# First expert round: stream 0's sum and the head of the rope jobs begin five half tiles later, the head runs at 2.45 positions a half tile, and three gathers are set three positions apart

## The reference, cut to what matters

```
x = x + encoder(layernorm(x))        # 4 layers: attention with ALiBi mask, feed-forward; final layernorm
x = x + experts(layernorm(x))        # first round
x = x + rope_attention(layernorm(x))
x = x + experts(layernorm(x))        # second round

def experts(x):                      # 8 experts, each token goes to its best 2
    comb = softmax weight of each token's two experts, else 0
    h = gelu(x @ W1[e] + b1[e]);  y = h @ W2[e] + b2[e]
    return sum over e of comb[e] * y[e]
```

## Time and profile before

| | |
|---|---|
| median of 3 runs | 2651.41 us (2651.28 to 2651.97) |
| the profiled execution | 2659.2 us, its span 2657.4 us |
| mean granted TensorE clock | 0.932 |
| PE / DVE / ACT / POOL busy | 86% / 66% / 55% / 39% of the span |
| second group of the first round, with the head | some 170 us, to about 1944 us |

### The profile page before, as it was taken

The page is one execution under the profiler, slowest core; times in us unless marked ns, Lnnn a source line. Parts: engine busy times, 40 slices in busy tenths (PEclk is TensorE's granted clock), DMA queues, the critical chain, the costliest instruction groups (busy, mean ns, idle before and its releaser), DMA issues.

```text
span 2657.4 us, 102576 instructions
## 1 busy us (share of the span) xinstructions
PE 2277.5 (86%) x44398; PEld 1394.7 (52%) x44398; DVE 1755.3 (66%) x5525; ACT 1463.5 (55%) x2646; POOL 1037.8 (39%) x1261
## 2 busy tenths in 40 slices
PE   3689999999999999999998888996878778888983
PEld 1345555555555555555554444785644444436872
DVE  6877777777777777777877774422567777852212
ACT  0357677777677777777655556442245434454441
POOL 6334333333334333333444545423334554442135
PEclk9799999999999999999988988998888888889997
DMA  4253333342433333333222211575622222205773
GB/s 115 81 161 101 109 120 117 105 132 93 121 107 105 124 105 116 109 128 93 87 68 62 75 33 34 185 220 147 177 67 70 65 64 62 64 13 173 224 205 109
DMA packets 162531, 288.76 MB, mean 109 GB/s; under 512 B 28504, under 2 KB 116312, under 8 KB 160344
## 3 DMA queue, kind: packets, MB, share of 16 engines
q1 hardware_dynamic: 153696, 264.23, 33.0%
q0 software_dynamic: 8384, 17.97, 2.5%
HBM read 227.33 MB, written 95.96 MB: 122 GB/s over the span
## 4 chain that ended last, share of the span: by engine, by line
PE 61%; DVE 19%; ACT 7%; issue 4%; POOL 3%; SPq 2%; DMA 2%; another core or an unknown queue 2%; POOLq 0%; ACTq 0%; DVEq 0%
PE bank L481 23%; PE bank L647 9%; PE bank L601 9%; DVE mx L1281 6%; PE bank L787 5%; PE bank L797 5%; PE bank L665 3%; ACT big L878 3%; PE bank L488 2%; DVE xn L973 1%; DVE stats L960 1%; ACT OT L884 1%; PE bank L609 1%; ACT big L946 1%
## 5 line engine op out<-in xcount | busy, mean ns | idle before, releaser
L878 ACT ACTIVATE big<-bank 128x512 f32<-128x512 f32 x1600 | 919.8, 599 | 704.5 <-PE bank L481 662.5
L1281 DVE TENSOR_REDUCE mx<-bank 128x16 f32<-128x512 f32 (+1 forms) x1440 | 903.0, 654 | 417.1 <-PE bank L609 385.0
L1577 POOL TENSOR_SCALAR_AFFINE_SELECT big<-big 128x768 f32<-128x768 f32 (+1 forms) x640 | 392.9, 637 | 915.5 <-ACT big L878 915.1
L481 PE MATMUL bank<-QS,KS 99*32 99x512 bf16 (+3 forms) x10240 | 651.6, 312 | 46.1 <-ACT big L878 35.3
L601 PE MATMUL bank<-KS,QS 96*32 96x352 bf16 (+15 forms) x10240 | 592.5, 294 | 103.2 <-DVE mx L1281 63.4
L647 PE MATMUL bank<-big,V 128*9 128x512 f32 (+3 forms) x5120 | 457.8, 453 | 19.0 <-POOL big L1577 10.7
L601 PEld LDWEIGHTS bank<-KS,QS 96*32 96x32 bf16 x10240 | 243.1, 99 | 410.7 <-issue 177.3
L481 PEld LDWEIGHTS bank<-QS,KS 99*32 99x32 bf16 x10240 | 218.0, 99 | 220.4 <-ACT big L878 94.0
L609 PE MATMUL bank<-mask_a,ident_b 128*32 128x64 bf16 (+1 forms) x5760 | 305.8, 196 | 0.8 <-issue 0.5
L946 ACT ACTIVATE big<-bank,big 128x256 f32<-128x256 f32 x368 | 150.7, 471 | 253.4 <-PE bank L787 198.8
L647 PEld LDWEIGHTS bank<-big,V 128*9 128x9 f32 x5120 | 130.8, 92 | 154.7 <-issue 86.2
(11 more groups left out here) (216 smaller groups left out, 2727.4 us busy)
## 6 DMA issues: line engine op xcount, KB each, us to landing
big<-e_pack SPq DMA_DIRECT2D x92, 578.0 KB
QS<-part_scr SPq DMA_DIRECT2D x480, 96.0 KB
KS<-part_scr SPq DMA_DIRECT2D x480, 96.0 KB
part_scr<-parts SPq DMA_DIRECT2D x80, 384.0 KB
x_rows<-in_alibi SPq DMA_DIRECT2D x47, 384.0 KB, 4.9
y_rows<-in_alibi SPq DMA_DIRECT2D x47, 384.0 KB, 5.6
big<-x_rows SPq DMA_DIRECT2D x92, 128.0 KB
y_rows<-big SPq DMA_DIRECT2D x92, 128.0 KB
```

The costliest lines, as they stand in the source:

```text
L481: last = mm(out[c:c + 32], stationary[:, c:c + 32], moving, start=start, stop=stop)
L878: A(dst, src, ACT.Exp).then_inc(exp_done, 1)
L1281: v.tensor_reduce(mx[:, quad, k, 0:w], src, axis=AX.X, op=ALU.max).then_inc(a_used, 1)
L1577: g.affine_select(out=blocks, in_=blocks, compare_op=ALU.is_ge, fill=0.0, base=0, pattern=[[0, n], [1, P]], channel_multiplier=-1).then_in ...
```

## The change

Five numbers. The head's lag goes from 8 to 13 half tiles and its rate from 2.1 to 2.45 positions a half tile; stream 0's sum and layernorm go from q = 7 to q = 12; the gathers of streams 1, 2 and 3 begin at positions 12, 30 and 12 where they began at 15, 36 and 16, with three positions from pair to pair where there was one.

```diff
-HEAD_LAG, HEAD_RATE = 8, 2.1
+HEAD_LAG, HEAD_RATE = 13, 2.45
...
-        COMBINE_FROM, COMBINE_EVERY, COMBINE_BESIDE = (7, 12), (6, 6), (1, 4)
+        COMBINE_FROM, COMBINE_EVERY, COMBINE_BESIDE = (12, 12), (6, 6), (1, 4)
...
-        GATHER = {1: (-2, 15, 1), 2: (-2, 36, 1), 3: (-1, 16, 1), 4: (0, 16, 5), ...
+        GATHER = {1: (-2, 12, 3), 2: (-2, 30, 3), 3: (-1, 12, 3), 4: (0, 16, 5), ...
```

More of the change, by code:

```diff
@@ L431, in hybrid_kernel @@
         ROUTE = ENC - JOBS
-        COMBINE_FROM, COMBINE_EVERY, COMBINE_BESIDE = (7, 12), (6, 6), (1, 4)
+        COMBINE_FROM, COMBINE_EVERY, COMBINE_BESIDE = (12, 12), (6, 6), (1, 4)
         GATHER_BESIDE = {1 + 6 * S + at: (S, k) for S in range(5) for k, at in enumerate((0, 1, 3, 4))}
         COMBINE = {1: (-2, 27), 2: (-1, 8), 3: (-1, 28), 4: (1, 15), 5: (2, 15), 6: (3, 15), 7: (4, 15)}
-        GATHER = {1: (-2, 15, 1), 2: (-2, 36, 1), 3: (-1, 16, 1), 4: (0, 16, 5), 5: (1, 18, 5), 6: (2, 18, 5), 7: (3, 18, 5)}
+        GATHER = {1: (-2, 12, 3), 2: (-2, 30, 3), 3: (-1, 12, 3), 4: (0, 16, 5), 5: (1, 18, 5), 6: (2, 18, 5), 7: (3, 18, 5)}
         def spread(j):
```

## The result

| | kernel before | changed kernel |
|---|---|---|
| median of the comparison, us | 2650.18 (2641.03 to 2651.97, 6 runs) | 2632.49 (2629.34 to 2637.97, 6 runs) |
| ratio, 95% interval | | 0.9943 [0.9924, 0.9962] |
| profiled execution, its span, us | 2659.2, 2657.4 | 2633.4, 2631.6 |

The change is faster by 15.1 us (0.0057 x 2650.2; interval 10.1 to 20.1). The forecast was 2645.1 with a range from 2638.0: the direction was right, the size less than half of what came, and the median lies 5.5 us under the range. Two later groups of runs gave 0.9932 for the same kernel.

The account below looks back on a forecast made before the run. PE was taken to be held by a 15.63 us wait for stream 0's sum, then by idle times before and behind the first scores; 9.3 - 2.0 - 4.0 - 0.9 + 3.9 = 6.3 us saved, 2645.1 us, range 2638.0 to 2651.5.

Parts of the forecast that it names:

- fifth term: Behind the first scores: fewer gathers of streams 2 and 3 beside dense work save 3.9 us, ends 0 and 7.5.
- 12.4 - 8.5 = 3.9: Two rows of eight priced 12.4 us; rows of six, four and two priced 4.9, 2.5 and 1.1; saving 3.9.
- third term: From L488 to the first scores: the front gets no shorter, so 3.7 us are given back plus 0.3, -4.0.
- fourth term: Ahead of the stacks' loads: ten gathers in one row, two more than before, cost a third of 2.5 us, -0.9.
- first, five half tiles into the hole: PE's idle time before L488: five half tiles of 1.87 us run inside the wait for stream 0's sum, +9.3 us.
- second, the sum begins later: Stream 0's sum on DVE: three more tiles' biases and a later gather landing start it 2.0 us later, -2.0.
- the remaining 21.5: In the front, behind the bias ahead of the last split: splits, store, landing and loads keep their 21.5 us.
- Both new waits: In the denser head: the third projection waits for DVE's read, 0.9 us, and V for the fourth rotation, 1.3.
- about 6: Sign for the fifth term: idle times beside stream 2's and 3's gathers fall from 9.3 us to about 6.
- short rows are free: Rival, chance 0.15: only the row of six costs and the front gets shorter; 12.1 us saved, 2639.3.
- The gathers hold nobody back: Rival, chance 0.20: the stops belong to the stacks' loads, not the gathers; 3.8 us saved, 2647.6.
- The slower case, by full DMA engines: Rival, chance 0.07: crowded transfers cause the stops, stream 0's gather lands 8.3 us late; -5.5 us, 2656.9.

Follow-up runs that it names:

- e9: The kernel before with the head at rate 2.45 up to its first scores (two half tiles from front to rest); ratio 0.9998 to the kernel before.
- e1: The changed kernel with the gathers of streams 1 to 3 back in the old rows of eight; ratio 0.9974 to the kernel before.
- e2: The kernel before with only the new gather places of streams 1 to 3, sum and head unchanged; ratio 0.9947 to the kernel before.
- e5: The changed kernel without the 24 gathers of streams 1 to 3 and their sums' waits; ratio 0.9906 to the kernel before.
- e7: The changed kernel with gather pairs of streams 1 to 3 at places of their own, no row over four in the rest; ratio 0.9944 to the kernel before.
- e6: The kernel before with the 24 gathers of streams 1 to 3 replaced by plain transfers of the same size and places; ratio 0.9933 to the kernel before.
- e15: The changed kernel with all eight gathers of stream 2 in one row behind the power; ratio 0.9954 to the kernel before.

## Why the prediction was right and wrong

Two steps failed, both towards too little: in the fifth term the prices behind "12.4 - 8.5 = 3.9", where the runs show 10.2, and in the third term the chain whose parts "keep their length", where it lost some 2 us. Together with the fourth term's 0.9 they make 10.1 of the 10.7 us by which the forecast fell short of the stage's 17.0. Step by step, with the mean of the three profiles of the change against the one of before:

| term | predicted | shown |
|---|---|---|
| first, five half tiles into the hole | +9.3 | taken as is, 2 out of the front, 3 out of the rest |
| second, the sum begins later | -2.0 | -1.4 (L488 19.9, 19.0, 18.9 us after the gather; 17.9 before) |
| third and fourth, the front | -4.9 | -1.1 (42.6 to 40.0, so 2.6 gained of the 3.7 counted) |
| fifth, gathers beside dense work | +3.9 | +10.2 (88.7 to 72.9, less 5.6 for three half tiles) |
| sum | 6.3 | 17.0 in the stage; 15.1 [10.1, 20.1] by the times |

**First and second term: right.** The hole filled with tiles; the wait for L488 fell to 1.82 us ("about 3" was forecast, "near 1815" was 1809 since the whole execution ran 5.5 us earlier). The biases beside the gather took 11.9 us for two, as the earlier trace rows had said (6.01 + 5.84), though one by one they were 4.65 and 7.26, and the gather landed 4.6 us after its last issue, between the two bounds of 2.6 and 5.5.

**Third term: wrong, by its step "the remaining 21.5 are splits, store, landing and loads, which keep their length".** Both new waits came (0.81 and 1.11 us, priced 0.9 and 1.3), but the front was 40.0 us in the mean, not 42.9. Up to the bias ahead of the last split the three profiles took 19.7, 19.7 and 22.3 us, where the step had 21.1 + 0.3 = 21.4; behind it they took 19.3, 20.2 and 18.7, where it kept 21.5. So 2.1 of the 2.9 us lie in the chain behind that bias. SyncE's first load of the stacks shows where:

```profile
1843.68 0.83 SPq L1694 DMA_DIRECT2D QS<-part_scr  x1
...
1839.02 0.83 SPq L1694 DMA_DIRECT2D QS<-part_scr  x1
```

From there to the first scores it was 11.7 us before (1855.34) and 9.2 in the change (1848.19), 10.0 and 9.3 in its other two profiles. Of the two half tiles that left the front one had stood behind that bias, where seven stood and six are left; that the chain shrank because of it is argued, not shown. e9, which makes only the front dense, gains 1.9 us of front, and e3, the change at the old rate, has one of 42.1. Both say that the denser head does shorten the front, though the fronts of one kernel differ by 2 us.

The spread ahead of the bias goes with the clock. PE's first tile matmuls behind L488, before, in the change, and in its third profile with their L488:

```profile
1813.60 3.05 PE L797 MATMUL bank<-big 128*128 128x128 f32 x16
...
1809.68 1.89 PE L787 MATMUL bank<-big 128*128 128x256 f32 x8
...
1804.60 1.09 PE L488 MATMUL bank<-ident,xn 128*128 128x128 f32 x4 [3.11 <-DVE xn L973]
1805.48 3.62 PE L787 MATMUL bank<-big 128*128 128x256 f32 x8
```

Behind the wait of 1.82 us L488 took 0.63 us and the up behind it 1.89; behind one of 3.11, in the same kernel, 1.09 and 3.62, and the front's clock was 0.87 in place of 0.95. The step had left the slow first matmuls that followed the old wait of 15.63 us in its 21.1.

**Fourth term: not decided.** The row of ten was given a third of 2.5 us. e1, whose row there is eight long, has a front of 39.9, which shows no cost. e2, which regroups alone, has one of 45.1, 2.5 over the kernel before; 1.3 of that lie ahead of the bias, at a lower clock (0.84 for its front), and 1.2 behind. Profiles of one kernel differ by as much in either part.

**Fifth term: the right mechanism at the wrong price.** This was the step "12.4 - 8.5 = 3.9". The two rows of eight cost more than the 12.4, namely 13.8 by e5 or 16.5 without e5's new wait; the short rows cost less than the 8.5 (4.9 for six, 2.5 for four and 1.1 for two), namely 3.6 or 6.3. Either way the difference is 10.2. The idle time beside the two gathers, "about 6" by the prediction's signs, was 3.2. The price for six came from tiles in the second round, which is work of another kind, and four was set between by rule of three. The chance of "short rows are free" was 0.15; by e7 rows of two and four can be free.

Of the 15.8 us by which the rest shrank, 5.6 are half tiles, 5.2 PE's idle time (10.7 to a mean of 5.5) and 5.0 busy time beyond the half tiles. By the mean granted clock the clock took 78.0 x 0.10 = 7.8 us of the busy time before and 67.4 x 0.07 = 4.7 now, so some 3 of those 5 are the clock's (an estimate); the other 2 are not explained.

**The rivals.** "The gathers hold nobody back" falls by e2, e5 and e6: the stacks' and tiles' loads stay and the stops go. The slower case, by full DMA engines, falls by e6: at a DMA share of 0.97 PE doesn't stop at all. On the Trainium skill's rule ("SBUF — State Buffer", section "Who interferes with whom": PE and ACT never wait on anyone): with plain transfers it agrees (PE 9.80 busy of 9.80); beside indirect ones it does not (6.80 of 12.00 in e15), whatever the reason; no run shows whether PE stands there for the SBUF at all. Loads of the stacks ran beside both stops of the earlier trace rows too, and it took e6 to tell the two apart.

Open: why an indirect row holds the other engines. The profile shows no semaphore that ends PE's idle times there, and the runs only show that the form matters, and that the price rises faster than the row's length.

## What to carry to other kernels

In this kernel indirect transfers issued in long rows beside dense work cost the other engines, not POOL. In a kernel that has such rows, look for idle times that end by "issue" or "remote" on several engines at once, a few us after a row begins, and try the same bytes as a plain transfer to see what there is to win. Break the rows up or put them where the end is set by a chain rather than by the engines; then look at once for the next wait, which here was the stacks' loads. Price a stop by its idle time and the clock that is lost with it, and take the price from work of the same kind at the same row length.

## What the runs showed that was not expected

- Two rows of eight indirect transfers beside scores cost 13.8 us, counted against e5, with its wait for the second job's stacks; the same two rows, plain, left the rest at 72.2 - 5.6 = 66.6 us when counted with the change's half tiles, which is the 69.3 without any less its wait of 2.60.
- The DMA engines move less about an indirect row of eight (191 to 218 GB/s) than beside a plain one (296 and 313 GB/s) that the same engine issues.
- POOL issues eight plain transfers of 64 KB in 4.4 us (e6), eight indirect ones of the same size in 9.8 (1789.33 to 1799.15 in the change).
- The price isn't in proportion: four, two and six cost 3.6 us together (6.3 with the wait that they seem to cover), eight in place of four 7.8, eight in place of two and six 2.7.
